# In each unit of a state-space scan, TensorE's sum of an older unit moves ahead of its side work

## The chip, the cores and the metric

The kernel runs on one core of a Trainium2 chip. A core has five engines with instruction queues of their own: TensorE (PE), VectorE (DVE), ScalarE (ACT), GpSimd (POOL) and SyncE (SP, which here only issues transfers). They wait for each other through semaphores. The metric is the device time of one execution in microseconds, the median over runs.

## The reference, cut to what matters

Sixteen batch items of 256 tokens by 256 features pass through four layers, all in float32. Layer 0 holds two state-space scans over 512 channels with 16 states each (one of them backwards in time), layer 1 a third one, layer 2 softmax attention with 16 heads, layer 3 linear attention with 8 heads. The scans are the bulk of the work:

```python
def _ssm(u, Wdbc, Wdt, bdt, Alog, Dp):
    dbc = jnp.einsum('bse,re->bsr', u, Wdbc)
    dlt, Bm, Cm = jnp.split(dbc, [R, R + N], axis=-1)
    delta = jax.nn.softplus(jnp.einsum('bsr,er->bse', dlt, Wdt) + bdt)
    dA = jnp.exp(delta[..., None] * -jnp.exp(Alog))
    dBu = delta[..., None] * Bm[:, :, None, :] * u[..., None]
    def step(h, xs):
        dA_t, dBu_t, C_t = xs
        h = dA_t * h + dBu_t
        return (h, jnp.einsum('ben,bn->be', h, C_t))
    ...
    return ys + u * Dp
```

## The kernel before

**Units.** A unit is one state n of one half (256) of the channels of one scan of one batch item. A batch item has 3 scans x 2 halves x 16 states = 96 units, the whole program 1536. A unit u passes through five stations. ACT (line 649, `dbut`) and POOL (line 658, `dbut`) each scale one half of the tokens of delta*u by B. PE transposes the result with four matmuls into one of two PSUM banks (line 574, `ps_b`, function `spread_b`; "the fill"). ACT computes `decay` (line 639). DVE runs the scan over time (line 678, `hst`). POOL multiplies by C (line 693, `g`). PE transposes g back with four matmuls and adds it into `ps_y` (line 602, function `sum_states`; "the sum"). When the 16 states of a half are summed (for layer 0, of both scans), ACT copies `ps_y` out (line 628, semaphore y_taken); the first sum of the next group waits for that copy, and ahead of it PE adds u itself (line 583).

**Buffers.** There are two banks of ps_b, three buffers each of hst and g, and four each of decay and dbut. So the fill of unit u waits for the scan of u-2 and for both parts of dbut, g of unit u waits for the scan of u and for the sum of u-3, and the scan of u waits for g of u-3.

**Ticks.** Each engine's queue is written out as a list of ticks, one unit each. At tick t PE fills for unit t+2 and sums unit t-2 (`LAG`). POOL does dbut for unit t+3 and then g of unit t. All other work (projections, norms, attention, the preparation of the next scans) is cut into small pieces, "side work". A table, `PLACES`, gives the tick of every piece on every engine within a period of 96 ticks, and `tick(t)` issues those that are due. Some ticks have none, some have several: at tick 6 of a period PE does twelve matmuls for the output projection of layer 1 (line 771) and then eight at line 1091. A piece may begin with a wait, and it may also end with one, which then holds what follows in the queue.

**Startup of a batch item.** SP loads the tokens (x_in, line 900) and, directly behind, three rows of modulation factors, spread over all partitions (row_in, line 901). DVE takes statistics of the tokens, ACT turns the variance into a scale, and DVE scales with it and with the rows (lines 913 and 915).

Of the kernel before, what the change touches and what calls it, by code (L numbers as in the profile page):

```python
# [176 lines left out]
def build(nc, dram, out):  # L177
    with ExitStack() as ctx:
# [6 lines left out]
        S = {n: ctx.enter_context(nc.semaphore(n)) for n in SEMS}  # L185
# [42 lines left out]
        with ExitStack() as pro:  # L228
            stage_sems, S = S, dict(zip(FIRST, S.values()))
# [183 lines left out]
        S = stage_sems  # L413
# [70 lines left out]
        def nth(sem, b, value):  # L484

            return b * EACH.get(sem, 1) + value
# [21 lines left out]
        class Scans:  # L508
# [48 lines left out]
            def tensor(self, pe, tick):  # L557
                for t in range(TICKS):
                    if t in self.unit:
                        for u in self.ahead(self.unit[t], B_AHEAD):  # L560
                            self.spread_b(pe, u)
                    tick(t)
                    if t - LAG in self.unit:
                        self.sum_states(pe, self.unit[t - LAG])

            def spread_b(self, pe, u):

                pe.wait_ge(S["dbu_a"], u + 1)
                pe.wait_ge(S["dbu_p"], u + 1)
                if u >= 2:  # L570
                    pe.wait_ge(S["scan_done"], u - 1)
                for e in range(HALF):
                    for t in range(TB):
                        last = nc.tensor.matmul(ps_b[:, u % 2, e * T + t * P:e * T + (t + 1) * P],  # L574
                                                dbut[:, u % NDBU, t, e * P:(e + 1) * P], ident[:, :],
                                                is_transpose=True, start=True, stop=True)
                last.then_inc(S["b_full"], 1)
# [147 lines left out]
        def norm_stats(ch, b, name, src):  # L725
            slot = NORMS.index(name)
            for t in range(TB):
                last = ch.mark(nc.vector.bn_stats(st[:, slot, t, :], src[:, t, :]))
            ch.eng.wait_ge(ch.sem, last)
            for t in range(TB):  # L730
                last = nc.vector.bn_aggr(mv[:, slot, t, :], st[:, slot, t, :])
            last.then_inc(S[f"var_{name}"], 1)
# [8 lines left out]
        def norm_scale(dve, b, name, scale_shift):  # L741
            slot = NORMS.index(name)
            dve.wait_ge(S[f"inv_{name}"], nth(f"inv_{name}", b, 1))
            for t in range(TB):
                last = scale_shift(t, mv[:, slot, t, 0:1], nrm[:, slot, 1, t:t + 1])
            return last

        def plain(src, dst):

            def go(t, mean, inv):  # L750
                return nc.vector.tensor_scalar(dst[:, t, :], src[:, t, :], mean, inv, ALU.subtract, ALU.mult)
            return go
# [154 lines left out]
        def l0_in_vector(dve, ch, b, at):  # L907
            yield next(at)
            dve.wait_ge(S["x_in"], nth("x_in", b, 16))
            dve.wait_ge(S["row_in"], nth("row_in", b, 16))  # L910

            def modulate(t, mean, inv):
                ch.done(nc.vector.scalar_tensor_tensor(out=xa[:, t, :], in0=x0[:, t, :], scalar=mean,
                                                       in1=rows_bc[:, 0, :], op0=ALU.subtract, op1=ALU.mult))
                return nc.vector.scalar_tensor_tensor(out=xa[:, t, :], in0=xa[:, t, :], scalar=inv,
                                                      in1=rows_bc[:, 1, :], op0=ALU.mult, op1=ALU.add)

            norm_stats(ch, b, "a1", x0)
            yield next(at)
            ch.done(norm_scale(dve, b, "a1", modulate))  # L920
            norm_stats(ch, b, "a2", xa)
            yield next(at)
            norm_scale(dve, b, "a2", plain(xa, xn_b)).then_inc(S["xn_a"], 1)
            yield next(at)
            dve.wait_ge(S["xn_a"], nth("xn_a", b, 1))
            ch.done(nc.vector.tensor_tensor(xa[:, :, :], xa[:, :, :], rows_bc[:, 2, :].unsqueeze(1).broadcast_to([P, TB, D]),
                                            ALU.mult))
            yield next(at)
            nc.vector.tensor_tensor(x0[:, :, :], x0[:, :, :], xa[:, :, :], ALU.add).then_inc(S["x0_done"], 1)
# [678 lines left out]
        with nc.Block() as block:  # L1608
# [36 lines left out]
            @block.vector  # L1645
            def _(dve):
                ch = Chain(dve, S["dve_chain"])
                scans.vector(dve, Between("DVE", {
                    "l0_in": lambda b, at: l0_in_vector(dve, ch, b, at), "l0_post": lambda b, at: l0_post_vector(dve, ch, b, at),
                    "prep0": lambda b, at: prep_vector(dve, ch, b, 0, A, 0, at),  # L1650
                    "prep1": lambda b, at: prep_vector(dve, ch, b, 1, B_, T - 1, at),
                    "prep2": lambda b, at: prep_vector(dve, ch, b, 2, B_, 0, at),
                    "l1_post": lambda b, at: l1_post_vector(dve, ch, b, at), "l1_in": lambda b, at: l1_in_vector(dve, ch, b, at),
                    "l2a": lambda b, at: l2a_vector(dve, ch, b, at),
                    "l2b": lambda b, at: l2b_vector(dve, ch, b, at), "l2_tail": lambda b, at: l2_tail_vector(dve, ch, b, at),
                    "l3": lambda b, at: l3_vector(dve, ch, b, at)}))
# [96 lines left out]
```

## Time and profile before

| | |
|---|---|
| median of 3 runs | 3688.07 us (3681.33 to 3688.27) |
| the profiled execution | 3710.73 us, its span 3709.0 us |
| steady stretch used here | 600 to 3200 us |
| PE / ACT / POOL / DVE busy there | 2407.8 / 2283.6 / 2250.5 / 2228.7 of 2600 us |

The profile is one execution, recorded by the hardware. Times of rows are microseconds from the start of the span. PE is TensorE's matmuls, PEld its weight loads. Matmuls of a group overlap in the pipeline: a group of four at 128x128 shows 0.60 us from the first start to the last end, while the next group's matmuls start about 0.44 us after its own start. The chain of waits goes back from the last instruction to what released it each time; an idle time stands with the engine that was idle and what ended it.

### The profile page before, as it was taken

The page shows a single profiled execution, that of the slowest core. Times are in us where ns is not written, and L with a number is a line of the kernel's source. Part 1 is how long each engine was busy: PE and PEld are TensorE (multiplying, and loading weights), DVE is VectorE, ACT ScalarE, POOL GpSimd, SP SyncE. Part 2 cuts the span into 40 slices and gives each one's busy share as a digit, 9 for nine tenths or more (in the row PEclk, how much of TensorE's full clock was granted, in tenths as well). Part 3 has the DMA queues.
Part 4 walks back from the last instruction along what each step waited for, and adds up shares of the span by engine and source line. Part 5 has one row for each costly group of instructions (what it writes and reads, how often), then busy time and mean ns, then how long its engine had stood idle before and what let it go on. Part 6 is the DMA issues. An engine that isn't in the chain of part 4 may idle for free.

```text
span 3709.0 us, 64650 instructions
## 1 busy us (share of the span) xinstructions
PE 3242.9 (87%) x22078; PEld 2674.0 (72%) x22078; DVE 2851.3 (77%) x3590; ACT 2921.7 (79%) x6624; POOL 2833.8 (76%) x3087
## 2 busy tenths in 40 slices
PE   6677788899999999999999999899989999897876
PEld 2556667787777878787877778787877777675643
DVE  1568778889797979798887979798888979793621
ACT  1658878888889898888888898988988898873522
POOL 0578989888898889888888888888888889780500
PEclk8899999999999999999999999999999999997866
DMA  4112222222122222212221222212221222220100
GB/s 170 59 51 82 80 66 65 85 65 88 61 87 63 83 63 80 74 59 89 65 87 58 82 69 79 71 60 89 63 88 60 87 61 78 60 69 19 44 2 10
DMA packets 140951, 257.08 MB, mean 69 GB/s; under 512 B 15921, under 2 KB 33329, under 8 KB 140225
## 3 DMA queue, kind: packets, MB, share of 16 engines
q1 hardware_dynamic: 140626, 252.95, 22.0%
q8 instruction: 179, 2.93, 0.3%
q14 instruction: 146, 1.20, 0.1%
HBM read 233.16 MB, written 5.05 MB: 64 GB/s over the span
## 4 chain that ended last, share of the span: by engine, by line
PE 48%; ACT 22%; DVE 11%; POOL 6%; issue 6%; DMA 0%; SPq 0%; POOLq 0%; DVEq 0%; ACTq 0%
PE ps_b L574 10%; PE ps_y L602 9%; ACT decay L639 8%; POOL g L693 5%; DVE hst L678 4%; PE ps_x L771 4%; ACT dbut L649 4%; PE ps_x L1276 3%; PE ps_x L765 3%; PE ps_v L765 3%; PE ps_x L1301 2%; PE ps_v L771 2%; PE ps_x L774 2%; PE ps_v L790 2%; ACT pT L1355 2%
## 5 line engine op out<-in xcount | busy, mean ns | idle before, releaser
L693 POOL TENSOR_TENSOR g<-hst,c_bc 128x512 f32<-128x512 f32 x1536 | 1976.1, 1287 | 482.2 <-PE ps_y L602 349.0
L678 DVE TENSOR_TENSOR_SCAN hst<-decay,ps_b 128x512 f32<-128x512 f32 x1536 | 1832.7, 1211 | 399.0 <-PE ps_b L574 231.8
L639 ACT ACTIVATE decay<-delta,acoef 128x256 f32<-128x256 f32 x3072 | 1378.4, 498 | 56.8 <-DVE hst L678 56.4
L574 PE MATMUL ps_b<-ident,dbut 128*128 128x128 f32 x6144 | 951.9, 278 | 241.4 <-DVE hst L678 110.3
L658 POOL TENSOR_TENSOR dbut<-dut,bcm 128x256 f32<-128x256 f32 x1536 | 972.4, 633 | 190.7 <-ACT dut L864 190.7
L602 PE MATMUL ps_y<-ident,g 128*128 128x128 f32 x6144 | 943.0, 276 | 20.8 <-ACT u L965 17.4
L574 PEld LDWEIGHTS ps_b<-ident,dbut 128*128 128x128 f32 x6144 | 708.0, 143 | 333.3 <-ACT dbut L649 165.1
L602 PEld LDWEIGHTS ps_y<-ident,g 128*128 128x128 f32 x6144 | 734.6, 142 | 147.4 <-issue 55.5
L649 ACT ACTIVATE dbut<-dut,bcm 128x256 f32<-128x256 f32 x1536 | 767.4, 500 | 22.0 <-PE ps_b L574 18.8
L1355 ACT ACTIVATE pT<-ps_x 128x1024 f32<-128x1024 f32 x128 | 129.5, 1012 | 74.5 <-PE ps_x L1311 64.3
L1301 PE MATMUL ps_x<-qT,kT 18*128 18x256 f32 x1024 | 159.6, 433 | 16.7 <-ACT pT L1355 15.6
L1384 DVE TENSOR_REDUCE mxt<-ps_x 128x4 f32<-128x1024 f32 x128 | 153.7, 1201 | 18.7 <-PE ps_x L1276 18.7
L1276 PE MATMUL ps_x<-kT,qT 17*128 17x256 f32 x1024 | 155.4, 423 | 6.5 <-DVE mxt L1384 4.5
L628 ACT ACTIVATE xm<-ps_y 128x512 f32<-128x512 f32 x64 | 38.2, 597 | 127.2 <-PE ps_y L602 127.1
L765 PE MATMUL ps_v<-xt_a,weights 128*128 128x256 f32 x512 | 133.2, 395 | 3.7 <-DVE yg L1080 2.4
L1301 PEld LDWEIGHTS ps_x<-qT,kT 18*128 18x128 f32 x1024 | 95.3, 200 | 56.9 <-ACT pT L1355 27.9
L765 PE MATMUL ps_x<-xt_x,weights 128*128 128x256 f32 x512 | 133.3, 391 | 2.7 <-ACT xt_x L1331 2.2
L771 PE MATMUL ps_v<-weights,yg 128*128 128x256 f32 x512 | 133.0, 401 | 1.6 <-DVE yg L1036 0.9
L1276 PEld LDWEIGHTS ps_x<-kT,qT 17*128 17x128 f32 x1024 | 92.9, 195 | 38.4 <-issue 24.2
L790 PE MATMUL ps_v<-u,weights 128*112 128x256 f32 x384 | 97.1, 390 | 25.1 <-ACT u L1137 24.2
L871 DVE SCALAR_TENSOR_TENSOR delta<-ps_v,delta 128x512 f32<-128x512 f32 x96 | 64.4, 671 | 63.8 <-ACT delta L852 63.8
L771 PE MATMUL ps_x<-weights,xt_a 128*128 128x256 f32 x384 | 107.9, 407 | 4.6 <-DVE kmax L1541 1.9
(192 smaller groups left out, 4080.3 us busy)
## 6 DMA issues: line engine op xcount, KB each, us to landing
c_bc<-c_rows SPq DMA_DIRECT2D x768, 256.0 KB, 3.2
rows_bc<-mod_rows SPq DMA_DIRECT2D x16, 384.0 KB, 4.4
ada_w<-in_ada_w_dram SPq DMA_DIRECT2D x1, 5120.0 KB
weights<-in_weights_dram SPq DMA_DIRECT2D x1, 4832.0 KB, 34.8
x<-in_x_dram SPq DMA_DIRECT2D x16, 256.0 KB, 3.8
x0p<-x SPq DMA_DIRECT2D x16, 256.0 KB, 2.3
xr<-x SPq DMA_DIRECT2D x16, 256.0 KB, 2.3
x<-x SPq DMA_DIRECT2D x16, 256.0 KB, 3.6
```

The costliest lines, as they stand in the source:

```text
L574: last = nc.tensor.matmul(ps_b[:, u % 2, e * T + t * P:e * T + (t + 1) * P], dbut[:, u % NDBU, t, e * P:(e + 1) * P], ident[:, :], is_tran ...
L602: last = nc.tensor.matmul(ps_y[:, t, e * P:(e + 1) * P], g[:, u % NG, e, t * P:(t + 1) * P], ident[:, :], is_transpose=True, start=False, ...
L639: last = nc.scalar.activation(decay[:, u % (DA_AHEAD + 2), e, :], delta[s][:, eb, :], ACT.Exp, scale=acoef[:, s, eb, n:n + 1])
L649: nc.scalar.activation(dbut[:, u % NDBU, 0, :], dut[s][:, 0, hh * HALF * P:(hh + 1) * HALF * P], ACT.Copy, scale=bcm[s][:, 0, n:n + 1]).th ...
L658: nc.gpsimd.tensor_tensor(dbut[:, u % NDBU, 1, :], dut[s][:, 1, hh * HALF * P:(hh + 1) * HALF * P], bcm[s][:, 1, n:n + 1].broadcast_to([P, ...
L678: nc.vector.tensor_tensor_scan(line(hst[:, u % NHST, :, :].rearrange("p e t -> p (e t)")), line(decay[:, u % (DA_AHEAD + 2), :, :].rearran ...
L693: nc.gpsimd.tensor_tensor(g[:, u % NG, :, :], hst[:, u % NHST, :, :], c_bc[:, k % NCB * CHUNK + n % CHUNK, :].unsqueeze(1) .broadcast_to([ ...
L765: last = nc.tensor.matmul(dst, weight[:, k, m0:m0 + m], rhs[:, k, :], start=(k == 0), stop=(k == kb - 1))
L771: last = nc.tensor.matmul(dst, lhs[:, k, t * P:(t + 1) * P], weight[:, k, :], start=(k == 0), stop=(bias is None and k == kb - 1))
L1276: last = nc.tensor.matmul(bank(ps_x, j, TB)[:, q, :], qT[r:r + DH2 + 1, hb, q * P:(q + 1) * P], kT[r:r + DH2 + 1, hb, :], start=True, stop ...
L1301: last = nc.tensor.matmul(bank(ps_x, j % 2, 2)[:, j // 2, :], kT[r:r + DH2 + 2, hb, m * P:(m + 1) * P], qT[r:r + DH2 + 2, hb, :], start=Tr ...
L1355: nc.scalar.activation(pT[:, :, :, :].rearrange("p a t n -> p (a t n)"), ps_x[:, 0:2, :].rearrange("p a n -> p (a n)"), ACT.Exp).then_inc( ...
```

## The change

It has two parts. In PE's list of a tick, the sum of unit t-2 is now issued directly behind the fill for unit t+2, and the side work of the tick after both. In DVE's list, the wait for the modulation rows moves from ahead of the first statistics to ahead of the first scaling.

```diff
--- before.py
+++ after.py
@@ -559,9 +559,9 @@
                     if t in self.unit:
                         for u in self.ahead(self.unit[t], B_AHEAD):
                             self.spread_b(pe, u)
-                    tick(t)
                     if t - LAG in self.unit:
                         self.sum_states(pe, self.unit[t - LAG])
+                    tick(t)
 
             def spread_b(self, pe, u):
 
@@ -907,7 +907,6 @@
         def l0_in_vector(dve, ch, b, at):
             yield next(at)
             dve.wait_ge(S["x_in"], nth("x_in", b, 16))
-            dve.wait_ge(S["row_in"], nth("row_in", b, 16))
 
             def modulate(t, mean, inv):
                 ch.done(nc.vector.scalar_tensor_tensor(out=xa[:, t, :], in0=x0[:, t, :], scalar=mean,
@@ -917,6 +916,7 @@
 
             norm_stats(ch, b, "a1", x0)
             yield next(at)
+            dve.wait_ge(S["row_in"], nth("row_in", b, 16))
             ch.done(norm_scale(dve, b, "a1", modulate))
             norm_stats(ch, b, "a2", xa)
             yield next(at)
```

The first place is on PE, around the long side work of tick 6 in a steady period. L574 is the fill, L602 the sum, L771 and L1091 side work. Before:

```order
L574 MATMUL ps_b<-ident,dbut 128x128 [waits scan_done,dbu_p,dbu_a]
L574 MATMUL ps_b<-ident,dbut 128x128 x3
L771 MATMUL ps_v<-weights,yg 128x256 x6
L1091 MATMUL ps_v<-gather,xn_a 128x256 [waits xn_b]
L1091 MATMUL ps_v<-gather,xn_a 128x256 x3
L602 MATMUL ps_y<-ident,g 128x128 [waits g_ready]
L602 MATMUL ps_y<-ident,g 128x128 x3
L574 MATMUL ps_b<-ident,dbut 128x128 [waits scan_done,dbu_p,dbu_a]
```

The same place now:

```order
L574 MATMUL ps_b<-ident,dbut 128x128 [waits scan_done,dbu_p,dbu_a]
L574 MATMUL ps_b<-ident,dbut 128x128 x3
L602 MATMUL ps_y<-ident,g 128x128 [waits g_ready]
L602 MATMUL ps_y<-ident,g 128x128 x3
L771 MATMUL ps_v<-weights,yg 128x256 x6
L1091 MATMUL ps_v<-gather,xn_a 128x256 [waits xn_b]
L1091 MATMUL ps_v<-gather,xn_a 128x256 x3
L574 MATMUL ps_b<-ident,dbut 128x128 [waits scan_done,dbu_p,dbu_a]
```

The sum moved from behind the side work to ahead of it, and the next fill follows the side work directly.

The second place is on PE at ticks 65 and 66, where a new group of sums starts: L583 adds u and carries the wait for the copy out of ps_y (y_taken). Before:

```order
L602 MATMUL ps_y<-ident,g 128x128 [waits g_ready]
L602 MATMUL ps_y<-ident,g 128x128 x3
L574 MATMUL ps_b<-ident,dbut 128x128 [waits scan_done,dbu_p,dbu_a]
L574 MATMUL ps_b<-ident,dbut 128x128 x3
L771 MATMUL ps_x<-weights,xt_a 128x256 x2
L774 MATMUL ps_x<-wdt_bias,pick 128x256
L583 MATMUL ps_y<-ident,u 128x128 [waits y_taken,ud_done_2]
L583 MATMUL ps_y<-ident,u 128x128 x3
L602 MATMUL ps_y<-ident,g 128x128 [waits g_ready]
```

The same place now:

```order
L602 MATMUL ps_y<-ident,g 128x128 [waits g_ready]
L602 MATMUL ps_y<-ident,g 128x128 x3
L574 MATMUL ps_b<-ident,dbut 128x128 [waits scan_done,dbu_p,dbu_a]
L574 MATMUL ps_b<-ident,dbut 128x128 x3
L583 MATMUL ps_y<-ident,u 128x128 [waits y_taken,ud_done_2]
L583 MATMUL ps_y<-ident,u 128x128 x3
L602 MATMUL ps_y<-ident,g 128x128 [waits g_ready]
L602 MATMUL ps_y<-ident,g 128x128 x3
L771 MATMUL ps_x<-weights,xt_a 128x256 x2
```

Between the last sum of the old group (first row) and L583 there stood a fill and side work; now only the fill.

## Rows read from the trace of the kernel before

**Rows 1.** The page: busy time of each engine, and the chain that ended last
```profile
PE 3242.9 (87%) x22078; PEld 2674.0 (72%) x22078; DVE 2851.3 (77%) x3590; ACT 2921.7 (79%) x6624; POOL 2833.8 (76%) x3087
...
PE 48%; ACT 22%; DVE 11%; POOL 6%; issue 6%; DMA 0%; SPq 0%; POOLq 0%; DVEq 0%; ACTq 0%
```

**Rows 2.** Busy by stretch: us, PE PEld DVE ACT POOL, PEclk, DMA, GB/s
```profile
600.00:3200.00 2600.00, 2407.81 (x17283) 2033.24 (x17283) 2228.66 (x2792) 2283.62 (x5203) 2250.52 (x2438) 0.99 0.24 74
```

**Rows 3.** Groups by line, 600 to 3200 us: busy us, mean ns, idle before
```profile
L693 POOL TENSOR_TENSOR g<-hst,c_bc 128x512 f32<-128x512 f32 x1219 | 1570.1, 1288 | 349.5 <-PE ps_y L602 297.3 <-DVE hst L678 30.0 <-issue 14.4
L678 DVE TENSOR_TENSOR_SCAN hst<-decay,ps_b 128x512 f32<-128x512 f32 x1218 | 1451.5, 1210 | 279.6 <-PE ps_b L574 183.4 <-ACT decay L639 66.2 <-POOL g L693 13.7
L658 POOL TENSOR_TENSOR dbut<-dut,bcm 128x256 f32<-128x256 f32 x1219 | 774.3, 635 | 0.0
```

**Rows 4.** Waits, 600 to 3200 us: total us, times, longest us
```profile
POOL g L693 <- PE ps_y L602: 297.3, 236, 5.9
DVE hst L678 <- PE ps_b L574: 183.4, 210, 2.7
ACT xm L628 <- PE ps_y L602: 78.9, 39, 4.4
...
PE ps_b L574 <- POOL dbut L658: 19.2, 48, 1.3
...
DVE hst L678 <- POOL g L693: 13.7, 36, 0.8
```

**Rows 5.** Timeline, 1503 to 1510 us: start, us, instruction [idle before]
```profile
1503.66 0.63 PE L574 MATMUL ps_b<-ident,dbut 128*128 128x128 f32 x4 [1.41 <-DVE hst L678]
1504.12 2.76 PE L771 MATMUL ps_v<-weights,yg 128*128 128x256 f32 x12
...
1508.44 0.60 PE L602 MATMUL ps_y<-ident,g 128*128 128x128 f32 x4
...
1508.88 0.60 PE L574 MATMUL ps_b<-ident,dbut 128*128 128x128 f32 x4
1509.19 1.27 POOL L693 TENSOR_TENSOR g<-hst,c_bc 128x512 f32<-128x512 f32 x1 [3.65 <-PE ps_y L602]
1509.46 0.25 DVE L731 BATCH_NORM_AGGREGATE mv<-stats 128x2 f32<-128x6 f32 x2
1509.62 1.19 DVE L678 TENSOR_TENSOR_SCAN hst<-decay,ps_b 128x512 f32<-128x512 f32 x1
```

**Rows 6.** The chain in order of time, 1580 to 1600 us: start, us
```profile
1585.67 1.13 PE ps_x L771 x4
...
1597.93 0.44 PE ps_y L602 x4
...
1598.86 1.22 DVE hst L678
```

**Rows 7.** The chain, 1618 to 1632 us
```profile
1624.45 0.45 PE ps_x L774 x2
```

**Rows 8.** The chain, 1692 to 1700 us
```profile
1696.33 0.64 POOL dbut L658
...
1697.06 0.63 PE ps_b L574 x4
```

**Rows 9.** Timeline, 1635 to 1638 us, around a group's end
```profile
1635.47 0.60 PE L574 MATMUL ps_b<-ident,dbut 128*128 128x128 f32 x4
1635.67 0.60 ACT L628 ACTIVATE xm<-ps_y 128x512 f32<-128x512 f32 x1 [1.72 <-PE ps_y L602]
...
1637.20 0.60 PE L583 MATMUL ps_y<-ident,u 128*128 128x128 f32 x4
```

**Rows 10.** Timeline, 66 to 92 us, the first batch item
```profile
73.64 0.38 SPq L900 DMA_DIRECT2D x<-in_x_dram  x1
...
77.56 0.75 DVE L728 BATCH_NORM_STATS2 stats<-x 128x6 f32<-128x256 f32 x2 [5.63 <-DMA rows_bc<-mod_rows]
```

**Rows 11.** One line's instructions: L1522, ns min/median/max
```profile
L1522 DVE TENSOR_SCALAR gate<-gate x16: 293/1318/1328, 780.5 to 3667.7; 128x256 f32<-128x256 f32 x16
```

## The prediction

> **What bounds the kernel now.** I began with the page: its busy shares and its chain that ended last [rows 1]. No engine stands out. PE is busy 87% of the span, ACT 79%, DVE 77%, POOL 76%, and the chain runs through PE for 48%, ACT 22%, DVE 11% and POOL 6%. The start and the tail blur such shares, so next I took the stage table for 600 to 3200 us, steady work at a granted clock of 0.99 [rows 2]: PE 2408 of 2600 us (93%), ACT 88%, POOL 87%, DVE 86%. Four engines work almost without pause and hand units to each other through short buffers. In this stretch there are 1218 scans [rows 3], so a unit takes 2600/1218 = 2.13 us, and a period of 96 units (one batch through all layers) 205 us. The program has 15 such periods. POOL's own work in a unit is 1.29 us (g) + 0.63 us (dbut) = 1.92 us [rows 3], 90% of the unit.
>
> Third, the waits of that stretch, which has 2600/205 = 12.7 periods [rows 4]. POOL waits 297 us for the sums of PE: 23 us a period, by far the longest wait in the list, and the one that the change aims at. DVE waits 183 us for filled banks, ACT 79 us for the last sum of a group. PE itself waits only 19 us for POOL's dbut. So POOL's idle time is large, but it is nearly all slack: what comes back from POOL to the others late is small.
>
> Last, one place in detail [rows 5]. PE fills the bank at 1503.66, is in side work from 1504.12, and reaches the sum only at 1508.44. POOL waits 3.65 us and starts g at 1509.19. Meanwhile DVE was in other work: it aggregates statistics from 1509.46 and its next scan starts at 1509.62, only 0.14 us after the fill of 1508.88 (0.60 us long) ends.
>
> **The change part by part.** No matmul is added or removed; POOL, ACT and SP keep their order. Between two pieces of side work PE did "sum of unit t-2, fill for t+3"; now it does "fill for t+3, sum of unit t-1". Such a group of four matmuls occupies PE's issue for 0.44 us (the row at 1597.93 in [rows 6]). From this all signs follow. A sum reaches POOL earlier by its side work. A fill behind side work reaches DVE 0.44 us earlier. Side work behind a fill comes 0.44 us later. Where PE waits inside side work, a sum is now done beforehand.
>
> Can the earlier sum make PE wait for POOL? No: the fill that now precedes it needs dbut of unit t+2, which POOL computes after g of unit t-2. When the fill has been issued, that g is done. This term is zero, without a range.
>
> *POOL late for PE.* PE stops for dbut in [rows 8]: the chain leaves PE at 1696.33, where dbut begins, and is back on it with the fill at 1697.06. All such waits are 19.2 us, 1.5 us a period [rows 4]. POOL, no longer held in side work, is up to one unit ahead. But where it has run back to back for long it can be no faster than 1.92 us a unit. I take half: -0.75 us a period (ends 0 and -1.5).
>
> *PE waiting inside side work.* ACT releases PE at 1585.67, and from there the chain stays on PE until the fill behind the sum of 1597.93 lets DVE scan at 1598.86 [rows 6]. The sum that stood behind this side work is now finished while PE waits: -0.44. I saw a second such place (z1w) in a period: -0.88 in all (ends 0, since ACT or DVE may be next late, and -1.3).
>
> *POOL held in the long side work.* In [rows 5] POOL gains a unit, but DVE has little room: it is busy up to the scan at 1509.62, and then gains the 0.44 at most. I take -0.2 (ends +0.5 and -0.45).
>
> *The new wait.* The first sum of a group of 16 waits until ACT has copied the finished sum out of ps_y (y_taken). In [rows 9] PE issues the last sum, fills from 1635.47 to about 1635.91 (0.44), does its side work and comes to L583 at 1637.20; the copy ran from 1635.67 to 1636.27. Side work covered it. Now L583 stands directly behind the fill: 1636.27 - 1635.91 = 0.36 us, 0.4 with the signal. Queued behind the waiting instruction are side work and the next fill, so DVE waits too. The order has three such places in a period (a fourth has this wait in its side work already). I price two, as PE waits for others a little after the third: +0.8 (ends +0.3 and +1.2, more if ACT comes late).
>
> *Side work 0.44 later.* In [rows 7] the chain leaves PE through side work: its matmuls end at 1624.90 and ACT carries the chain on. There the sum ahead of side work is in the way: +0.44, and one lesser place: +0.5 (ends 0 and +0.9).
>
> *row_in.* The wait moves from the first statistics to the first scaling. DVE waited 5.63 us at 77.56 [rows 10], but x was itself issued only at 73.64, and rows_bc directly behind it on the same queue, so x lands hardly earlier: -0.4 us once (ends 0 and -3.9, all the time since its issue). The wait now stands behind the wait for inv_a1 and holds scans only if the rows are late, which no later batch shows.
>
> Sum: -0.75 - 0.88 - 0.2 + 0.8 + 0.5 = -0.53 us a period, times 15 = -8 us, with row_in -8.4. The profiled execution took 3710.73 us (span 3709.0) and would take 3702.3. It is 22.7 us above the median of the timed runs, 3688.07; to those the same difference gives 3688.07 - 8.4, rounded to 3679.
>
> **A rule that speaks against it.** DVE and POOL disturb each other here: scaling a 128x256 tile (L1522) takes 293 ns at best and 1318 ns in the median [rows 11], about as long as one g of POOL. The Trainium skill, SBUF — State Buffer, section "Who interferes with whom", says why: GpSimd shares a port pair with VectorE's two-port forms and with its instructions that have two SBUF inputs, and who comes second is blocked for the whole instruction of the first. By that rule POOL, working on through the side work, would block DVE's modulation there, which now finds it idle. The row agrees; whether it costs time is a rival below.
>
> **The rivals.**
> *More than I credit.* POOL's 297 us of waits are the largest of all, and with four engines this close each late buffer is passed on. If the dbut waits (1.5), DVE's waits for g (13.7 us, 1.1 a period [rows 4]), the two places of 0.44 and half a microsecond behind the long side work all come back, that is 4 us a period: -60, 3628. Against it: the chain has only 6% on POOL, and DVE was itself just in time.
> *Nothing.* PE's total work is the same and it is busy for 93%; the chain goes through long stretches where PE or ACT alone is full. POOL's idle time then only moves from sums to scans: 3688.
> *Slower through y_taken.* Its place is the three group starts. If the copy ends 0.6 us behind the fill rather than 0.4, each 0.6 delays fill and side work, and side work's extra 0.44 leaves PE at one of them: 3 x 0.6 + 0.44 = 2.2 us a period. If the gains come to nothing, +34: 3722; if half of them come, 3710, which I name. It decides from the point where PE is not waiting anyway at these starts. For: PE is full around 1635 [rows 9]. Against: 0.4 us is all that the row shows.
> *Slower through the shared port.* Where POOL now works through side work, DVE's scaling and modulation wait for a g. The excess in [rows 11] is 1.03 us an instruction; with one to two more such waits a period and the gains above: +1 net, +15: 3703. Against: POOL's total busy share hardly changes, so chances of a clash move rather than grow.
> *It does not do what it says.* If side work seldom stood between fill and sum, nothing would move. The waits speak against it.
>
> **How the numbers follow.** What a measurement of this kernel can tell from no change is 0.2%, 7.4 us. Forecast 0.33 (own range 3668 to 3684; 0.24 of it is faster, 0.09 within); more than I credit 0.21, all faster; nothing 0.17; y_taken 0.20 and shared port 0.07, slower; not as said 0.02, the same. Faster 0.45, same 0.28, slower 0.27. The range is 3640 to 3714: below it lies half of the large gain's case, above it a third of the y_taken case.
>
> **What would show it.** In the profile after: POOL's waits for L602 fall from 297 us towards 150 or less in the same stretch, and its wait of 3.65 us goes. PE's waits for dbut fall below 1 us a period. L583 shows a new wait for L628, some 0.4 us at two or three places a period. No sum waits for g. If POOL's waits fall and the time does not, POOL was slack; if L1522 and its like grow, it was the port. The forecast is wrong if the chain moves off PE and ACT, or if waits for y_taken are a microsecond or more.

## The result, and the profile after

The changed kernel took 3731.43 us in the median of 4 runs (3708.35 to 3739.34), the kernel before 3688.17 us on the same chip (4 runs, 3681.33 to 3690.99). The ratio is 1.0107 with a 95% interval of 1.0073 to 1.014: 1.1% slower, where the prediction had 3679 us and a range up to 3714. Every ratio below is to runs of the kernel before on the same chip in the same job. In the jobs of the experiments the kernel before took 3695.5 to 3701.93 us (medians of 17 to 29 runs). The four runs with a median of 3688.17 us are on the low side of that, so the 1.1% may be somewhat too large.

The profiled execution after took 3708.35 us (span 3706.6), the shortest of its four, and that of before 3710.73 us, 23 us above its median. The two spans hide the loss: behind the last of the periods compared here the trace of before is 19 us longer, and why is not known. So the traces are compared in the steady stretch, 600 to 3200 us, first by engine (us, then PE, PEld, DVE, ACT, POOL, granted clock, DMA share, GB/s), as in [rows 2]:

```profile
600.00:3200.00 2600.00, 2384.30 (x17142) 2015.62 (x17143) 2238.00 (x2776) 2260.99 (x5166) 2245.56 (x2415) 0.99 0.24 73
```

There are fewer instructions on every engine, and DVE is busy for longer all the same. The groups that answer to [rows 3], and the one that explains the rest:

```profile
L693 POOL TENSOR_TENSOR g<-hst,c_bc 128x512 f32<-128x512 f32 x1208 | 1555.5, 1288 | 354.4 <-PE ps_y L602 178.3 <-DVE hst L678 113.8 <-issue 44.2
L678 DVE TENSOR_TENSOR_SCAN hst<-decay,ps_b 128x512 f32<-128x512 f32 x1206 | 1432.0, 1210 | 261.3 <-PE ps_b L574 158.0 <-ACT decay L639 66.3 <-POOL g L693 21.8
L658 POOL TENSOR_TENSOR dbut<-dut,bcm 128x256 f32<-128x256 f32 x1207 | 781.6, 648 | 0.0
L1058 DVE COPY cols<-mod_cols 128x4 f32<-128x4 f32 x13 | 46.7, 3595 | 0.0
```

In the same 2600 us there are 1206 scans where there were 1218, 1.0% fewer, close to the loss of the timed runs. POOL waits 178.3 us for the sum and no longer 297.3, as predicted, but its idle time ahead of g is the same, 354.4 and 349.5 us: of the 119 us that it gained it now waits 84 more for DVE (113.8, before 30.0) and 30 more in "issue" (44.2, before 14.4). The last row is a copy of 128x4 numbers at tick 5 of each period. The trace of before has for the same row (ns min/median/max):

```profile
L1058 DVE COPY cols<-mod_cols x13: 1786/1798/1811, 677.4 to 3147.4; 128x4 f32<-128x4 f32 x13
```

and the trace after:

```profile
L1058 DVE COPY cols<-mod_cols x13: 3579/3599/3612, 671.4 to 3162.1; 128x4 f32<-128x4 f32 x13
```

Twice as long, in all 13 periods. The waits of the stretch (total us, times, longest us), to be held against [rows 4]:

```profile
POOL g L693 <- PE ps_y L602: 178.3, 151, 5.4
DVE hst L678 <- PE ps_b L574: 158.0, 194, 4.4
...
PE ps_b L574 <- DVE hst L678: 110.5, 91, 3.2
...
ACT xm L628 <- PE ps_y L602: 49.8, 27, 3.9
...
PE ps_b L574 <- POOL dbut L658: 16.1, 27, 0.8
...
PE ps_y L583 <- ACT xm L628: 10.8, 24, 0.6
```

PE waits 110.5 us for a scan to free a bank, 63.3 before, and its longest such wait is 3.2 us, before 1.8. Half of the increase comes from one place in each period, as will be seen (13 x 1.83 us = 24 us). Where these 3.2 us are, the timeline of one period shows (start, us, instruction, in brackets the idle time before and what ended it). Before, DVE and POOL around the copy:

```profile
1499.61 1.26 POOL L693 TENSOR_TENSOR g<-hst,c_bc 128x512 f32<-128x512 f32 x1
1499.68 1.80 DVE L1058 COPY cols<-mod_cols 128x4 f32<-128x4 f32 x1
...
1500.78 0.60 PE L602 MATMUL ps_y<-ident,g 128*128 128x128 f32 x4
1500.84 0.60 POOL L658 TENSOR_TENSOR dbut<-dut,bcm 128x256 f32<-128x256 f32 x1
...
1501.53 1.27 POOL L693 TENSOR_TENSOR g<-hst,c_bc 128x512 f32<-128x512 f32 x1
```

The copy begins 0.07 us after POOL's g and is held for that g and the dbut behind it. The dbut ends at 1501.44; the next g starts at 1501.53, because it needed the sum of 1500.78, which stood behind side work. In this pause of 0.09 us the copy runs and ends at 1501.48; the fill that needs the next scan comes at 1503.66 [rows 5]. After:

```profile
1920.31 1.29 POOL L693 TENSOR_TENSOR g<-hst,c_bc 128x512 f32<-128x512 f32 x1
1920.39 3.60 DVE L1058 COPY cols<-mod_cols 128x4 f32<-128x4 f32 x1
...
1921.54 0.63 POOL L658 TENSOR_TENSOR dbut<-dut,bcm 128x256 f32<-128x256 f32 x1
...
1922.11 1.28 POOL L693 TENSOR_TENSOR g<-hst,c_bc 128x512 f32<-128x512 f32 x1
1922.34 0.60 PE L602 MATMUL ps_y<-ident,g 128*128 128x128 f32 x4
1923.34 0.62 POOL L658 TENSOR_TENSOR dbut<-dut,bcm 128x256 f32<-128x256 f32 x1
...
1924.85 2.30 DVE L678 TENSOR_TENSOR_SCAN hst<-decay,ps_b 128x512 f32<-128x512 f32 x2
...
1926.17 1.27 POOL L693 TENSOR_TENSOR g<-hst,c_bc 128x512 f32<-128x512 f32 x1 [2.20 <-issue]
1926.18 0.98 PE L574 MATMUL ps_b<-ident,dbut 128*128 128x128 f32 x4 [3.24 <-DVE hst L678]
1926.95 1.06 PE L602 MATMUL ps_y<-ident,g 128*128 128x128 f32 x4
```

The sum is there in time now, so POOL's second g follows the first dbut without a pause, and the copy is passed over once more, until POOL has nothing to do because the scan, which stands behind the copy in DVE's queue, is missing. The scan is 1.80 us late and PE idles 3.24 us, before 1.41. The Trainium skill (SBUF — State Buffer, "Who interferes with whom") says that a copy may take the port pair shared with GpSimd, and that who comes second is blocked for the whole instruction of the first. The trace agrees and shows more: here it is blocked for four instructions of the other in a row.

A pause always let VectorE in, but it is not the only way. In both traces the scaling at L1522 waits for one g only (1.32 us, 12 of 12 periods), although POOL's dbut follows that g without a pause. I counted, over both steady stretches, the ends of POOL instructions that fall inside a copy or `tensor_scalar` of VectorE between tiles in SBUF. Where POOL then paused, VectorE's instruction was let through in 79 of 79 cases; where POOL did not pause, it was let through in 372 and passed over in 117. What decides there is not shown.

The chain of waits (start, us) goes through it, and shows a second loss behind it:

```profile
1920.47 3.52 DVE cols L1058
1923.99 0.67 DVE stats L728 x2
...
1926.18 0.98 PE ps_b L574 x4
1927.16 0.85 PE ps_y L602 x4
1928.01 3.50 PE ps_v L771 x12
```

The fill takes 0.98 us where it took 0.63, and the twelve matmuls of L771 3.5 to 3.7 us where they took 2.76 [rows 5]. The granted clock of these 5 us:

```profile
1926.18:1931.18 5.00, 5.00 (x20) 4.46 (x21) 4.93 (x8) 2.91 (x8) 3.90 (x4) 0.66 0.02 5
```

0.66 is a mean over the two levels of 1.2 and 2.4 GHz. In 11 of the 13 periods the clock fell there, to 0.66 to 0.73 in the 5 us, and L771 took 3.23 to 4.44 us; in the other two it stayed at 1.00 and L771 took 2.76. Before, it stayed at 1.00 in all 13. What the fall costs can be read inside this one trace: from the late fill to the next fill PE needs 6.53 to 6.91 us in the 11 periods and 5.22 us in the two (before: 5.22 in all 13). That is 1.35 us a period on average over the 13.

### The profile page after: what moved, and what is told of

Read it like the earlier page. It is cut to its first block, busy times and chain, and to the rows that moved or that the text cites. A ratio compares the mean times of both kernels' runs of the same rounds, so it can differ in the third digit from the quotient of the medians.

```text
span 3706.6 us, 64650 instructions
## 1 busy us (share of the span) xinstructions
PE 3219.0 (87%) x22078; PEld 2657.4 (72%) x22078; DVE 2874.9 (78%) x3590; ACT 2916.7 (79%) x6624; POOL 2848.8 (77%) x3087
## 4 chain that ended last, share of the span: by engine, by line
PE 47%; ACT 19%; DVE 12%; POOL 12%; issue 7%; DMA 0%; DVEq 0%; POOLq 0%; ACTq 0%
PE ps_b L574 10%; POOL g L693 9%; PE ps_y L602 9%; ACT decay L639 6%; DVE hst L678 5%; PE ps_x L771 4%; ACT dbut L649 3%; PE ps_x L765 3%; POOL dbut L658 3%; PE ps_v L765 3%; PE ps_x L1276 3%; PE ps_x L1301 2%; PE ps_v L771 2%; PE ps_v L809 2%; PE ps_x L774 2%
## 5 line engine op out<-in xcount | busy, mean ns | idle before, releaser
L574 PE MATMUL ps_b<-ident,dbut 128*128 128x128 f32 x6144 | 958.4, 279 | 271.2 <-DVE hst L678 164.4
L658 POOL TENSOR_TENSOR dbut<-dut,bcm 128x256 f32<-128x256 f32 x1536 | 986.8, 643 | 181.3 <-ACT dut L864 181.3
L574 PEld LDWEIGHTS ps_b<-ident,dbut 128*128 128x128 f32 x6144 | 712.2, 142 | 491.0 <-ACT dbut L649 214.0
L602 PE MATMUL ps_y<-ident,g 128*128 128x128 f32 x6144 | 933.2, 275 | 3.4 <-POOL g L693 2.7
L602 PEld LDWEIGHTS ps_y<-ident,g 128*128 128x128 f32 x6144 | 728.8, 142 | 6.1 <-POOL g L693 6.0
L1384 DVE TENSOR_REDUCE mxt<-ps_x 128x4 f32<-128x1024 f32 x128 | 154.4, 1206 | 19.0 <-PE ps_x L1276 18.3
L771 PE MATMUL ps_v<-weights,yg 128*128 128x256 f32 x512 | 142.7, 423 | 1.1 <-DVE yg L1036 0.9
L771 PEld LDWEIGHTS ps_v<-weights,yg 128*128 128x128 f32 x512 | 104.7, 217 | 21.2 <-issue 5.0
L771 PE MATMUL ps_x<-weights,xt_a 128*128 128x256 f32 x384 | 107.6, 406 | 4.6 <-DVE kmax L1541 1.9
```

Source lines behind the costliest of these rows:

```text
L602: last = nc.tensor.matmul(ps_y[:, t, e * P:(e + 1) * P], g[:, u % NG, e, t * P:(t + 1) * P], ident[:, :], is_transpose=True, start=False, ...
L658: nc.gpsimd.tensor_tensor(dbut[:, u % NDBU, 1, :], dut[s][:, 1, hh * HALF * P:(hh + 1) * HALF * P], bcm[s][:, 1, n:n + 1].broadcast_to([P, ...
L771: last = nc.tensor.matmul(dst, lhs[:, k, t * P:(t + 1) * P], weight[:, k, :], start=(k == 0), stop=(bias is None and k == kb - 1))
L1384: nc.vector.tensor_reduce(by_head[:, 2 * g_:2 * g_ + 2, :, DH2 + 1], ps_x[:, 0:2, :].rearrange("p j (q n) -> p j q n", q=TB), AX.X, ALU.ma ...
```

## The experiments

My theory after the two traces: the earlier sum closes a pause of POOL that VectorE's copy needed; the late scan and then the lowered clock cost more than the change gains. The rivals were the wait for y_taken, the moved wait for row_in, and that the late scan alone is the loss. Twelve kernels follow, each run 4 to 12 times and compared with the kernel before.

**The two parts of the change, each alone.** e1 has only PE's order, e2 only the moved wait (the two pieces of the diff above).

> Only PE's order is changed, the row_in wait stays where it was. Theory (the order makes it slower through VectorE's wait for the port that POOL holds): 1.008 to 1.012 of the kernel before, as the whole change. Rival (the moved row_in wait delays DVE): 1.000.

> Only the row_in wait is moved, PE's order as before. Theory: nothing but the start moves, 0.999 to 1.000. Rival (row_in): about 1.01. L1058 stays at 1.8 us in the steady stretch.

Measured: e1 3719.2 us, ratio 1.0048 (1.0029 to 1.0068), its copy 3.60 us; e2 3694.27 us, 0.9982 (0.996 to 1.0004), its copy 1.80 us. The loss comes with the order. e1 lost less than the whole change (1.0107, another job) and less than I expected. e2 does not explain this, and e1's trace is no better in the steady stretch (1200 scans, clock 0.98). The low four runs of before in the first job account for part of it at most; the rest stays open. The loss of the order alone is then between 0.5% and 1.1%.

**The copy in a form that does not take the port.** e3 (on the changed kernel) and e4 (on the one before):

```diff
-            nc.vector.tensor_copy(cols1[:, :].unsqueeze(2), mod_cols[:, 0:2 * DB, bass.ds(b, 1)])...
+            nc.vector.tensor_reduce(cols1[:, :], mod_cols[:, 0:2 * DB, bass.ds(b, 1)], AX.X, ALU.max)...
```

> The changed kernel, with the 128x4 copy of L1058 written as a tensor_reduce over an axis of one element (same values). Theory (the copy waits for POOL's port for two of POOL's pairs, 3.6 us, DVE holds the next scan, PE idles 3.2 us and its clock falls): L1058 takes 0.2 us, the idle of PE before the long side work shrinks from 3.2 us to under 1 us, the clock stays at 2.4 GHz there, and the time falls from 1.011 to 0.99 to 1.000 of the kernel before. Rival (the copy only sits where DVE waits anyway, the loss is in PE's order, by y_taken or by side work that comes later): 1.005 to 1.011.

> The control to the one before: the kernel before with the same reduce in place of the copy. There the copy took 1.8 us. Theory: up to 1.6 us a period back, 0.993 to 0.999. If it gains as much as the changed kernel does, the copy is a cost of both and not the cause of the difference.

Measured: e3 3675.8 us, 0.9926 (0.9898 to 0.9954); e4 3695.08 us, 0.9982 (0.996 to 1.0003). One instruction of 128x4 numbers turns the change from slower into faster; on the kernel before it brings 0.2%, within the noise. There the late fill came 1.6 us earlier too, but other instructions of VectorE grew (L1410 from 318 to 1222 ns, the scaling L751 of xn_b from 568 to 1053 ns). Beside the same g of POOL the reduction takes 0.15 us. But the port struck again at once, at the next instruction that takes it (e3, the same place):

```profile
1902.03 0.15 DVE L1058 TENSOR_REDUCE cols<-mod_cols 128x4 f32<-128x4 f32 x1
...
1905.28 2.76 PE L771 MATMUL ps_v<-weights,yg 128*128 128x256 f32 x12
1905.31 4.37 DVE L751 TENSOR_SCALAR xn_a<-x,mv,nrm 128x256 f32<-128x256 f32 x2
```

Two scalings take 4.37 us in place of 1.15: the first is passed over like the copy, while POOL runs four instructions without a pause. PE has the side work L771 meanwhile, and the clock holds. But the side work behind it needs the scaled tile, and PE waits for it in all 13 periods (total us, times, longest us):

```profile
PE ps_v L1091 <- DVE xn_a L751: 22.0, 13, 1.7
```

The late fill comes 3.4 us earlier after the copy's start than in the changed kernel, and the fill behind it 7.15 us later in place of 5.22. Part of the gain is thus given back.

**The pause given back.** e5 is the changed kernel, but at tick 4 of each period the side work stands ahead of the sum, as before (e5's lines are 5 higher):

```diff
+                    old = BASE[1] <= t < BASE[LAST] and (t - BASE[1]) % PERIOD in OLD_AT
+                    if old:
+                        tick(t)
                     if t - LAG in self.unit:
                         self.sum_states(pe, self.unit[t - LAG])
-                    tick(t)
+                    if not old:
+                        tick(t)
```

> The changed kernel with the old order at one tick of 96 (tick 4 of each steady period, where POOL's g behind the copy L1058 waited 0.08 us for the sum and let the copy have the port). The copy stays a copy. Port theory: L1058 is back at 1.8 us, PE idles 1.4 us and not 3.2 before the long side work, no fall of the clock there, 0.993 to 0.999 of the kernel before. Rival (the order as such costs the time, the copy is a symptom): 1.004 to 1.011, since 95 of 96 ticks are unchanged.

Measured: 3668.55 us, 0.9908 (0.9892 to 0.9923). Its timeline has the pause again:

```profile
1490.19 1.80 DVE L1063 COPY cols<-mod_cols 128x4 f32<-128x4 f32 x1
...
1491.34 0.62 POOL L663 TENSOR_TENSOR dbut<-dut,bcm 128x256 f32<-128x256 f32 x1
...
1492.04 1.27 POOL L698 TENSOR_TENSOR g<-hst,c_bc 128x512 f32<-128x512 f32 x1
...
1494.18 0.63 PE L579 MATMUL ps_b<-ident,dbut 128*128 128x128 f32 x4 [1.41 <-DVE hst L683]
```

0.08 us between dbut and g, the copy is back at 1.80 us, PE's wait at 1.41, and the clock at 1.00 in all 13 periods. The order of one tick in 96, with nothing else touched, is worth 2% (0.9908 against 1.0107, two jobs), or 1.4% against e1 (1.0048).

**The lateness by itself.** e6 is the kernel before, with a reduction of 128x1650 numbers added behind the copy (its result is not used), 1.86 us on DVE without the port.

> The kernel before with 1.8 us of other VectorE work (a tensor_reduce over 1650 elements of the weights into a scratch column, one SBUF input) directly behind L1058. Port theory says that what hurts is 1.8 us more on DVE ahead of the scan of tick 6: the idle of PE there goes from 1.4 to about 3.2 us, its clock falls in most periods, and the time is 1.006 to 1.012 of the kernel before. Rival (DVE has slack there): under 1.003.

Measured: 3743.19 us, 1.0108 (1.0092 to 1.0125). The copy stays at 1.81 us, PE's wait is 3.20 us, and the clock fell in 13 of 13 periods. So 1.86 us of lateness at this one place costs 1.1%, 40 us or 2.7 us a period: more than itself. The order of PE is not needed for the loss, only the late scan. The 2.7 us hold the lateness and the fallen clock together.

**Lateness and clock apart.** e11 is the changed kernel, but the fill at tick 5, just ahead of the wait, is done six times (24 matmuls in place of 4, the same values).

> The changed kernel, but the fill at tick 5 of each period in the steady stretch is written six times over (24 matmuls in place of 4, the same values), so that TensorE has about 2.2 us more to do just where it would idle 3.24 us; VectorE's copy of 128x4 stays at 3.6 us and the scan behind it is as late as in the changed kernel. Theory (the lost time is 1.8 us of lateness plus a clock fall behind the idle stretch): the granted clock stays at 1.00 in the 5 us behind, L771 x12 takes 2.76 us in place of 3.2 to 4.8, and the time falls to 1.000 to 1.006. Rival (the clock is a side show, the lateness of the scan alone costs the time): L771 x12 may be shorter but the time stays at 1.008 to 1.013.

Measured: 3694.53 us, 1.0 (0.9982 to 1.0019).

```profile
1912.14 3.59 DVE L1058 COPY cols<-mod_cols 128x4 f32<-128x4 f32 x1
...
1913.66 2.78 PE L574 MATMUL ps_b<-ident,dbut 128*128 128x128 f32 x24
...
1917.93 0.63 PE L574 MATMUL ps_b<-ident,dbut 128*128 128x128 f32 x4 [1.05 <-DVE hst L678]
1918.39 0.60 PE L602 MATMUL ps_y<-ident,g 128*128 128x128 f32 x4
...
1918.83 2.76 PE L771 MATMUL ps_v<-weights,yg 128*128 128x256 f32 x12
```

More work on PE made the kernel faster, by 1.1% as the two ratios stand. The copy is as long as in the changed kernel, and so is the time from its start to the late fill: 5.79 us (1912.14 to 1917.93), there 5.79 too (1920.39 to 1926.18). But the clock stays at 1.00 in 13 of 13 periods, L771 takes 2.76 us, and the periods are 205.3 to 206.2 us long, in the changed kernel 205.5 to 209.9. In the two periods shown VectorE and POOL also work at the same distances from the copy's start up to the late fill, to within 0.02 us, so the extra matmuls moved nothing else there. The traces side by side (us; the last column is the mean distance of late fills in the steady stretch):

| kernel | copy | its start to the late fill | late fill to next fill | clock held | period |
|---|---|---|---|---|---|
| before | 1.80 | 3.98 | 5.22 | 13 of 13 | 205.8 |
| e5 (pause at tick 4) | 1.80 | 3.99 | 5.22 | 13 of 13 | 204.4 |
| e11 | 3.60 | 5.79 | 5.22 | 13 of 13 | 205.8 |
| after | 3.60 | 5.78 | 6.53 to 6.91, 5.22 twice | 2 of 13 | 207.6 |
| e6 | 1.81 | 5.77 | 6.57 to 8.18 | 0 of 13 | 209.1 |
| e3 (reduction) | 0.15 | 2.39 | 7.15 | 13 of 13 | 205.4 |
| e9 (both repairs) | 0.15 | 2.42 | 5.19 | 13 of 13 | 201.3 |

From e5 to the changed kernel the place grows by 1.80 us of lateness and 1.35 us of lowered clock, 3.15 together, and the period by 3.1. e11 stands between the two, 1.4 us above the one and 1.8 below the other. So each of the two costs is roughly half of the loss; the split is not known better than to 0.4 us. The timed runs give 0.9% from e5 to e11 and 1.1% from e11 to the changed kernel (0.5% to e1).

**Is there more of the port?** e7 is the changed kernel and e10 the one before, both with all five of DVE's copies of small tiles (L1058, L1364, L1410, L1520, L1521) written as reductions.

> The changed kernel with all five small copies of VectorE (L1058, L1364, L1410, L1520, L1521) as tensor_reduce. In the changed kernel with only L1058 replaced these took 0.45 to 1.01 us each, of which about 0.3 to 0.85 is waiting. Port theory: 0.1 to 0.2 us each, 0 to 2 us a period back, 0.985 to 0.993 of the kernel before. Rival (DVE has slack at those places, or the wait moves on to the next tensor_scalar): as with L1058 alone, 0.990 to 0.995.

> Control for e7: the kernel before with all five copies as reductions, the order untouched. One copy alone gave 0.9982. The other four are 4 columns or less wide and took 0.3 to 1.8 us in before, so I expect 0.994 to 0.998. If this comes out at 0.989 as e7 did, then the reductions alone carry e7 and the change of order brings nothing; if it stays at 0.995 or above, the order brings the rest, about 0.6 to 0.8%, which is more than the 0.2% that the prediction's sum gave it.

Measured: e7 3664.25 us, 0.9889 (0.9869 to 0.9909); e10 3682.25 us, 0.9965 (0.9948 to 0.9983). The reductions bring 0.35% by themselves, and the changed order 0.76% on top (two jobs). In the kernel before, the other four copies took 0.32 to 0.54 us, not up to 1.8 as the expectation has it.

**The wait for y_taken.** e8 (with the one reduction) and e12 (with all five) have the side work ahead of the sum, as before, at the units that begin a group; the code is that of e5 with another condition:

```diff
+                    old = u is not None and self.units[u][2] == 0
```

> The changed kernel with L1058 as tensor_reduce and, at the first unit of each group of 16, the old order (side work, then the sum), so that L583 no longer stands directly behind the fill. In the kernel with the reduce alone L583 and its weight loads waited 22 us for the copy L628 in 2600 us, 0.9 us of PE a period. If these waits are on the path: 3 to 10 us faster than with the reduce alone (0.9926), 0.989 to 0.992. If they are covered: 0.992 to 0.995.

> As e7 (changed order, all five copies as reductions), but with the old order at the units that begin a group, so that the sum's new wait for VectorE's y_taken is no longer ahead of the side work. With e8 the copies at L1415 and L1371 were drawn out, which hid the answer; here they can't be. If the new wait lies on the path as the prediction had it (+0.8 us in 205), the time is 0.2 to 0.4% below e7: 0.985 to 0.987. If the wait costs nothing: 0.988 to 0.990. If what e8 lost was the sum that comes late at group starts and not its copies: 0.995 or more.

Measured: e8 3692.42 us, 0.9974 (0.9958 to 0.9989), slower than e3 (0.9926) and than either expectation. PE's waits for the copy L628 are gone, but VectorE's copy at L1415 grew from 1013 to 1778 ns, so it says nothing on y_taken; that this clash is the whole loss is not shown. (y_taken is ScalarE's signal; the second expectation names VectorE by mistake.) With the copies out of the way, e12 took 3664.82 us, 0.992 (0.9899 to 0.9941), against 3664.25 us and 0.9889 of e7, in two jobs. To take the waits away thus brought no gain: the 0.2 to 0.4% that the prediction's term would give did not appear, and by the ratios e12 is 0.3% slower. One trace of each points the other way (the periods average 203.7 us in e12 and 204.5 in e7), so this is not settled to better than 0.3%. The ratio lies between what I expected of a wait that costs nothing and of late sums that cost much.

**Both repairs.** e9 has the old order at tick 4 and all five reductions.

> Both repairs at once: the changed order with the old one at tick 4 of a period, and all five of VectorE's copies of small tiles (L1063, L1369, L1415, L1525, L1526) written as reductions, which in the runs so far took 0.15 us beside a busy POOL. If the whole loss of the change is the late copy, the two repairs cure the same thing and the time is that of the better one, 0.989 of before. If the old order at tick 4 also saves something else (the port instructions at ticks 6 to 11, which in the changed kernel were longer on average), they add: 0.984 to 0.987. Above 0.993 would say that the old order at tick 4 costs POOL time once the copy no longer needs its pause.

Measured: 3623.85 us (3623.22 to 3625.9), 0.9811 (0.9789 to 0.9832), below what I expected of any sum. The trace shows where it comes from: e7, like e3, still has the two scalings of 4.37 us behind the copy. With the old order at tick 4 they take 1.82 us, and the next fill comes 5.19 us behind the late one in place of 7.15. That is 1.9 us a period, the size of the 0.8% between e7 and e9. POOL does not pause at the scalings of e9; why they are let through there is not shown. By line in the steady stretch (busy us, mean ns), e7 and then e9:

```profile
L751 DVE TENSOR_SCALAR xn_a<-x,mv,nrm 128x256 f32<-128x256 f32 x50 | 75.5, 1549 | 0.0
```

```profile
L683 DVE TENSOR_TENSOR_SCAN hst<-decay,ps_b 128x512 f32<-128x512 f32 x1243 | 1475.5, 1208 | 256.2 <-PE ps_b L579 152.7 <-ACT decay L644 66.8 <-POOL g L698 21.6
...
L756 DVE TENSOR_SCALAR xn_a<-x,mv,nrm 128x256 f32<-128x256 f32 x52 | 44.1, 887 | 0.0
```

e9 does 1243 scans in 2600 us, before 1218: a period is 201 us. It is the fastest kernel of the study, 1.9% below before and, by the two ratios, 2.9% below the changed one.

## Why the prediction was wrong

**What was right.** PE's order does what the prediction said of it: POOL's waits for L602 fell to 178 us (forecast towards 150 or less), ACT's for the last sum from 78.9 to 49.8, no sum waits for g, and L583 shows the new wait for L628, 24 times, 0.6 us at most (forecast 0.4 us at two or three places). One sign failed: the wait of 3.65 us did not go. It moved to the next g, which now waits for the sum behind the same side work, 4.10 us at 1934.28 us and 2.42 us in a period whose clock held (2347.64 us). Cleared of the late copy, the order gains: e3 against e4 0.56%, e7 against e10 0.76%, e5 0.9%, that is 20 to 34 us. The sum had 8.

**The step that failed** is the rival "Slower through the shared port", given 0.07 and priced at +1 a period net, and the sentence that dismissed it: "POOL's total busy share hardly changes, so chances of a clash move rather than grow." The share did stay (2245.56 us of 2600, before 2250.52), and over the stretch the clashes did move rather than grow: without L1058, VectorE's copies and `tensor_scalar`s took 215.8 us together, before 222.1 (summed from the traces). A scaling that had been passed over by five instructions of POOL in 10 of 12 periods is now passed over by one at most. Before and after (busy us, mean ns):

```profile
L751 DVE TENSOR_SCALAR xn_a<-rows_bc,mv,nrm 128x256 f32<-128x256 f32 x24 | 51.7, 2193 | 0.0
```

```profile
L751 DVE TENSOR_SCALAR xn_a<-rows_bc,mv,nrm 128x256 f32<-128x256 f32 x24 | 25.7, 1111 | 0.0
```

What failed is to take the sum for the cost. Several clashes grew and several shrank, and each costs by its place: the one at L1058, 1.80 us longer in each period, lies ahead of the scan that PE waits for, in front of the long side work, and e6 shows that 1.86 us there cost 1.1%. The sum of the prediction had nothing for it. It grew because the change removed the pause of POOL that had let the copy in (e5). I priced a clash at one g, 1.03 us, from the median of [rows 11]; L1522 itself did not change (1322 ns). The copy at L1058 lay at tick 5, next to the place that I studied [rows 5], and I never looked at its 1.80 us for 512 numbers, which were the warning that it already waited for POOL.

**The step that was missing** is the clock. I let every lateness cost its own length. The wait of 1.41 us ahead of the fill [rows 5] stood in my rows, and 1.8 us more made it one behind which the clock fell. The traces of e5, e11 and the changed kernel put this at 1.35 to 1.8 us a period, about as large as the lateness itself.

**The new wait**, +0.8 a period: PE waits 10.8 us there in 12.7 periods, 0.85 a period, so its size was right, but taking it away brought no gain in the timed runs (e12 against e7). Whether it is on the path is not settled at this size; it is not the cause of the loss, since e5 and e3 keep the wait (11.5 us) and are faster than before. The rival that ended slower through y_taken fell with that.

**POOL late for PE**, -0.75: the waits for dbut fell from 19.2 to 16.1 us, 0.24 a period and not half of 1.5. **PE waiting inside side work**, **POOL held in the long side work** and **side work later** were not measured one by one. Their sum with the others must be larger than forecast: e3 and e5 gain two to four times as much, and in the traces of e5 and before, which are alike at the copy, the period falls by 1.4 us where 0.53 was forecast. Where the rest comes from is not shown; a candidate is the scaling above, which is as short in e5 (1109 ns). In e9 the whole gain is 1.9%, near the rival "More than I credit" (3628), though that is with repairs which the change doesn't have.

**row_in**, -0.4 once: e2's interval includes no change. In the traces the first scaling starts 5.56 us after the load of x is issued in the kernel before (73.64 to 79.20), and 4.52 us after it in the changed one (70.15 to 74.67).

```profile
74.67 0.48 DVE L912 SCALAR_TENSOR_TENSOR xa<-x,mv,rows_bc 128x256 f32<-128x256 f32 x1 [0.68 <-DMA rows_bc<-mod_rows]
```

As forecast the wait is now here, 0.68 us in the first batch item.

## What to carry to other kernels

Where two engines share a port, look for instructions that take far longer than their size before changing anyone's order, and ask what pause lets them through: an order that makes the other engine smoother may close it. Ask of each clash where it lies, not only what all of them sum to: here the sum fell and the one ahead of TensorE's wait grew. Price a wait on TensorE not by its length alone, but also by the granted clock behind it, and compare it with the longest wait behind which the clock still held. When a reorder is slower than its sum, look for the one tick that turns it before giving up the whole: here one of 96 did.

## What the runs showed of the hardware

- A copy of 128x4 numbers took 1.80 us behind one g and one dbut of GpSimd, and 3.60 us behind two of each; as a reduction 0.15 us. Pauses of GpSimd of 0.08 and 0.09 us let this copy through; where GpSimd's next instruction followed at once, it was passed over. Two scalings of 128x256 took 1.15, 1.82 or 4.37 us for waits of the same kind. No pause of GpSimd (79 of 79 cases in the two traces) failed to let an instruction of VectorE in; without a pause 372 were let in and 117 passed over.
- Behind waits of TensorE of 1.05 to 1.42 us at this place the granted clock was 1.00 in every period (before, e5 and e11, 39 periods). Behind waits of 3.18 to 3.25 us it fell in 11 of 13 (after), 12 of 13 (e1) and 13 of 13 (e6), and the twelve matmuls of L771 took up to 5.3 us in place of 2.76. In the second batch of e11 (484.49 us), ahead of the steady stretch, it was at 0.66 behind a wait of 2.02 us.
- At a granted clock of 1.00 the twelve matmuls took 2.76 us, at 0.50 (e6, from 1525.19 us) 5.30 us, 1.9 times as long. In the changed kernel PE needed 1.3 to 1.7 us more from the late fill to the next where the clock fell (11 periods against 2 of the same trace).
